# Packing the row-maximum search into 18 visits a group, moving its pairs behind the second products of two chunks, and warming the entries of three stages, in a gated attention and MLP kernel on one Trainium2 core

## The reference, cut to what matters

```python
def reference(x, w_qkv, w_out, W1, B1, W2, B2, LN_G, LN_B):   # x: (4, 1024, 256) float32
    xn = layernorm(x)
    # attention: 16 heads of 16 dims, causal, over 4 sequences of 1024
    q, k, v = split(xn @ w_qkv); q = q / 4
    scores = where(causal, q @ k.T, -1e10)
    s = (softmax(scores) @ v) @ w_out
    # MLP: 6 blocks, hidden width 1024
    y = xn
    for i in range(6):
        y = gelu(y @ W1[i].T + B1[i]) @ W2[i].T + B2[i] + y
        if i < 5: y = layernorm(y) * LN_G[i] + LN_B[i]
    return x + s * silu(y)
```

## Time and profile before

| what | us |
|---|---|
| median of three runs | 1572.16 |
| the profiled execution, its own time | 1569.95 |
| span of its records | 1568.2 |
| PE busy in the span | 1539.3 (98%) |
| DVE busy | 1227.6 (78%) |
| ACT busy | 959.3 (61%) |
| POOL busy | 384.8 (25%) |

### The profile page before, as it was taken

One profiled execution on the slowest core, in us unless ns is written; L12 is line 12 of the kernel. 1 busy time (PEld: TensorE's weight loads), 2 busy tenths in 40 slices (PEclk: granted clock), 3 DMA queues, 4 the chain that ended last, 5 costly groups with the idle time before them and its releaser, 6 DMA issues. The chain is left out here.

```text
span 1568.2 us, 28737 instructions
## 1 busy us (share of the span) xinstructions
PE 1539.3 (98%) x10960; PEld 1196.9 (76%) x10960; DVE 1227.6 (78%) x2688; ACT 959.3 (61%) x1404; POOL 384.8 (25%) x325
## 2 busy tenths in 40 slices
PE   7989999999999999999999999999999999999998
PEld 6879888888888888888888888888888644444443
DVE  7835988888889888879898898887666487777742
ACT  4455655565555555555656555555545599898985
POOL 2002322222212222223222222221110222333333
PEclk9999999999999999999999999999999899999999
DMA  9868546547545214232132142131610355456441
GB/s 309 319 204 243 152 122 181 151 119 195 138 118 114 69 36 115 66 93 69 47 102 69 44 115 66 38 103 53 186 56 28 108 143 170 141 180 180 114 133 45
DMA packets 110145, 193.37 MB, mean 123 GB/s; under 512 B 13644, under 2 KB 80716, under 8 KB 102348
## 3 DMA queue, kind: packets, MB, share of 16 engines
q1 hardware_dynamic: 110008, 191.54, 42.3%
HBM read 136.70 MB, written 79.95 MB: 138 GB/s over the span
## 5 line engine op out<-in xcount | busy, mean ns | idle before, releaser
L759 ACT ACTIVATE m_hid<-m_h_ps,m_b1s 128x512 f32<-128x512 f32 x384 | 264.7, 689 | 490.4 <-PE m_h_ps L862 456.2
L834 DVE TENSOR_TENSOR m_hidl<-m_hid,m_hidh 128x512 fp32r<-128x512 f32 x384 | 358.7, 938 | 184.4 <-ACT m_hidh L762 173.5
L1093 ACT ACTIVATE a_prob<-a_st_ps 128x1024 f32<-128x1024 f32 x288 | 277.6, 1023 | 36.1 <-PE a_st_ps L1164 31.4
L875 PE MATMUL m_y_ps<-shared,m_hidh 128*128 128x256 f32 x1536 | 273.8, 281 | 0.5 <-DVE xres L793 0.5
L762 ACT ACTIVATE m_hidh<-m_h_ps,m_b1s 128x512 fp32r<-128x512 f32 x384 | 261.6, 681 | 0.0
L862 PE MATMUL m_h_ps<-xth,shared 128*128 128x512 f32 x768 | 254.3, 392 | 3.7 <-ACT m_hidh L762 2.0
L875 PEld LDWEIGHTS m_y_ps<-shared,m_hidh 128*128 128x128 f32 x1536 | 234.8, 188 | 19.0 <-issue 14.6
L875 PE MATMUL m_y_ps<-w2h,m_hidh 128*128 128x256 f32 x768 | 219.0, 285 | 0.7 <-DVE xres L793 0.7
L875 PE MATMUL m_y_ps<-w2l,m_hidh 128*128 128x256 f32 x768 | 212.7, 277 | 0.0
L875 PE MATMUL m_y_ps<-shared,m_hidl 128*128 128x256 f32 x768 | 212.7, 277 | 0.0
L875 PE MATMUL m_y_ps<-w2h,m_hidl 128*128 128x256 f32 x768 | 212.7, 277 | 0.0
(11 more groups left out here) (116 smaller groups left out, 2583.8 us busy)
## 6 DMA issues: line engine op xcount, KB each, us to landing
turned_rows<-apart SPq DMA_DIRECT2D x47, 512.0 KB, 2.7
apart<-turned_rows SPq DMA_DIRECT2D x188, 128.0 KB, 3.1
mq<-q_stacks SPq DMA_DIRECT2D x16, 896.0 KB, 6.9
mk<-k_stacks SPq DMA_DIRECT2D x16, 896.0 KB, 10.1
shared<-k_stacks SPq DMA_DIRECT2D x14, 896.0 KB
shared<-q_stacks SPq DMA_DIRECT2D x14, 896.0 KB
q_stacks<-q_parts SPq DMA_DIRECT2D x96, 128.0 KB
k_stacks<-k_parts SPq DMA_DIRECT2D x96, 128.0 KB
```

What stands on the lines that cost most here:

```text
L759: nc.scalar.activation(hid[n % 2][:], h_ps[n % 2][:], ACT.Gelu, bias=b1s[i % 2][:, k:k + 1])
L834: nc.vector.tensor_tensor(hidl[n % 4][:], hid[n % 2][:], hidh[n % 4][:].bitcast(F32), ALU.subtract).then_inc(low_done, 1)
L875: m = nc.tensor.matmul(y_ps[:, j, :], h[n % 4][:, j * P:(j + 1) * P], w[par][:, k, :], start=(k == 0 and j % 2 == 0 and h is hidh and w is ...
L1093: nc.scalar.activation(to, scores, ACT.Exp).then_inc(exp_done, 1)
```

## The change

It has these parts.

1. `max_pieces` packs two pieces with a diagonal into one visit where they fit in a buffer: 18 visits a group, with the same matmuls and the same reductions. 189 visits, in 95 places, are in stage 2, and 115 in stage 3, over the same 124 steps (none shares a step).
2. In stage 2 PE takes a place's pair behind `down(n-2)`, `down(n-1)`, and DVE takes it one chunk later.
3. The six products of `up` stand in another order.
4. Stage 1: the weights come in three column parts; PE does 16 transposes of `ident` ahead of `transpose0` and 12 behind it; the biases of MLP block 0 are loaded here; the Gelu table is asked for here, and the one for Exp at the end of stage 2's ACT list.
5. Stage 3: in steps 0 and 1, where there are no `values` yet, PE does four matmuls of 512 columns for nothing (`keep_awake`); `values` waits for each diagonal apart; of the last eight output tiles the first goes ahead of the last `values`, and four use the score buffers, so that tiles 1 to 5 wait for no earlier one.

```diff
 def max_pieces():
...
-    pieces = []
-    for qt in range(QT):
-        for half in range(1 + qt // HG):
-            keys = min(P * (qt + 1) - BANK * half, BANK)
-            columns = min(BANK // keys, PAIR)
-            pieces += [(qt, half, c, columns, keys) for c in range(0, PAIR, columns)]
-    return pieces
+    def own(qt, c, col=0):
+        return qt, qt // HG, c, P * (qt % HG + 1), col
+
+    def far(qt, c):
+        return qt, 0, c, BANK, 0
+
+    both = range(PAIR)
+    pieces = [[own(2, c), own(0, c, BANK - P)] for c in both] + [[own(1, c, BANK // 2 * c) for c in both]]
+    pieces += [[own(3, c)] for c in both] + [[far(4, c)] for c in both]
+    pieces += [[own(6, c), own(4, c, BANK - P)] for c in both] + [[far(5, c)] for c in both]
+    pieces += [[own(5, c, BANK // 2 * c) for c in both]] + [[far(6, c)] for c in both]
+    return pieces + [[far(7, c)] for c in both] + [[own(7, c)] for c in both]
...
 def project(nc, x, wqkv, w1t, w2t, b1, b2, scratch, keep):
-        WCOLS = [slice(0, 2 * DIM), slice(2 * DIM, 3 * DIM)]
+        WCOLS = [slice(DIM * part, DIM * (part + 1)) for part in range(3)]
...
+            load_bias(sp, keep, b1, b2, 0)
...
             low(0)
             split_w(1)
+            split_w(2)
             statistics(1)
...
+            act.preload_act_table(ACT.Gelu)
             high_w(0)
             high(0)
             high_w(1)
+            high_w(2)
...
+            def keep_awake(times):
+                for j in range(times):
+                    nc.tensor.transpose(v_ps[:, 0, 0:P], ident[:], ident[:])
+
+            keep_awake(16)
             transpose0()
+            keep_awake(12)
...
 def mlp(...):
-            load_bias(0)
...
-            act.preload_act_table(ACT.Gelu)
...
+            act.preload_act_table(ACT.Exp)
...
-                for v in AT.get(n, ()):
+                for v in AT.get(n - 1, ()):
                     search.dve_visit(dve, s_ps[v % 2], v)
...
-                for c in range(HALVES):
-                    for w, x in ((w1h, xth), (w1h, xtl), (w1l, xth)):
+                products = ((w1h, 0, xth), (w1h, 0, xtl), (w1l, 1, xth), (w1l, 0, xth), (w1h, 1, xtl), (w1h, 1, xth))
+                for order, (w, c, x) in enumerate(products):
...
-                for v in AT.get(n, ()):
-                    search.pe_visit(pe, s_ps[v % 2], v, 2)
                 if n >= 2:
                     down(n - 2)
                     down(n - 1)
+                for v in AT.get(n, ()):
+                    search.pe_visit(pe, s_ps[v % 2], v, 2)
...
 def output_schedule():
-            at, bank = copied_at(N_GROUPS - 1, 1) + 3 + k // 2, ("s", k % 2)
+            at = copied_at(N_GROUPS - 1, 1) + (3 + k if k else -1)
+            bank = (("s", 0), ("s", 1), ("st", 0), ("st", 1), ("st", 2), ("st", 3), ("s", 0), ("s", 1))[k]
...
 def attend(...):
-            act.preload_act_table(ACT.Exp)
...
+                    if P * kt == lo:
+                        selected += 1
+                        pe.wait_ge(masked, selected)
...
+            def keep_awake():
+                for j in range(HG):
+                    nc.tensor.matmul(o_ps[0][2 * HD * j:2 * HD * (j + 1), :], va[0][:, 0, j, :], xres[:, 0:2, :], start=True, stop=True,
+                                     skip_group_check=True)
...
+                if at < LATE:
+                    keep_awake()
```

More of the change, by code:

```diff
@@ L188, in pe_visit @@
             pe.wait_ge(s.loaded[m % 2], 2 * 16 * (m // 2 + 1))
-        qt, half, first, columns, keys = PIECES[p]
-        for c in range(columns):
+        for part, (qt, half, c, keys, col) in enumerate(PIECES[p]):
             for side in range(2):
-                if c == 0 and before > 0:
+                if part == 0 and before > 0:
                     pe.wait_ge(s.maxed, before - 1 + side)
                 rows = slice(SIDE * side, SIDE * side + STACK)
-                i = s.nc.tensor.matmul(s_ps[:, side, c * keys:(c + 1) * keys], s.q[m % 2][rows, first + c, qt * P:(qt + 1) * P],
-                                       s.k[m % 2][rows, first + c, half * BANK:half * BANK + keys], start=True, stop=True)
+                i = s.nc.tensor.matmul(s_ps[:, side, col:col + keys], s.q[m % 2][rows, c, qt * P:(qt + 1) * P],
+                                       s.k[m % 2][rows, c, half * BANK:half * BANK + keys], start=True, stop=True)
         i.then_inc(s.done, 1)
```

48 lines of the change are left out of this document (27 added, 21 removed).

## The result

The changed kernel takes 1563.09 us (median of four, 1562.50 to 1566.81); the kernel before, run beside it, 1572.03. The ratio is 0.9948, with a 95% interval from 0.9935 to 0.9961: 0.5% faster where 0.9% was forecast, 1563.1 where 1557.5 stood, inside the range (1554 to 1563.5) by 0.4 us and far from its centre. The profiled execution took 1563.66 us with a span of 1561.8; before 1569.95 and 1568.2. So of 14.7 us forecast 6.4 appear in the span. Where they went can be read place by place.

What follows compares the result with a forecast made beforehand. It took PE's instructions to bound stage 2 and ACT's exponents ordinary stage 3 steps. Terms −4.0 + 0.7 − 2.0 − 4.4 − 3.3 − 1.7 gave −14.7 us: 1555.2 profiled, 1557.5 median, range 1554 to 1563.5 (8 in 10).

Steps and rivals of the forecast that it cites:

- start of stage 1: Transposes of group 1 come later because DVE's list has two weight splits ahead of the statistics: +0.7 us, bounds +0.3 and +0.7.
- entry −2.0: Entry of stage 2: with biases and Gelu table loaded early, PE no longer waits before the third chunk: −2.0 us.
- packing −4.0: Stage 2: ten of 105 places go, each costing 0.40 us beyond its columns: −4.0 us.
- place 0: Stage 2: moving the pair behind the second products costs nothing, taken as 0 within −4 to +4 us.
- entry of stage 3: Earlier table load saves 0.8 us and idle matmuls holding the clock save 3.65 us: −4.4 us.
- doubles in stage 3: No step has two visits any more, so steps 41 and 82 lose no time on ACT: −3.3 us.
- the end: Last output tiles: PE ends near 1562, then POOL's seven adds set the end at 1563.9: −1.7 us.
- the clock of stage 3 falls anyway: Rival: the entry of stage 3 gives +1.0 us instead of −4.4, total 1562.9 us; chance 0.20.
- a wait for the buffers: Rival: in stage 2 PE waits for DVE's late reductions in some 32 places, 1570 to 1589 us; 0.07 slower, 0.07 about even.
- rounds with a pair over 6.4 us: Sign that the forecast is wrong: stage 2 rounds with four 512-column matmuls were to still take 6.35 us.
- the rival that they wake it: Rival: stage 1's transposes raise PE's clock, so the start loses 0.3 us and not 0.7, total 1557.1 us; chance 0.12.
- the places give nothing back: Rival: in stage 2 the new place costs 0.04 us more, 95 times, eating packing's 4.0 us, total 1561.5 us; chance 0.10.

Runs made afterwards that it cites:

- best: Changed kernel with column loads ahead of the search's DMAs, group 1's statistics ahead of two weight splits, 8 idle transposes before group 1's transposes: 1557.03 us.
- no_packing: Changed kernel with the 20 pieces a group of the kernel before, instead of 18: 1567.59 us, ratio 0.9979.
- control: The changed kernel run once more, nothing edited: 1561.15 us, ratio 0.9933.
- stage3_cold: Changed kernel without the eight idle matmuls in steps 0 and 1 of stage 3: 1564.03 us, ratio 0.9953.
- columns_first: Changed kernel with the four column loads of every slot issued ahead of the search's loads and stores on SP: 1557.93 us, ratio 0.9906.
- start_cold: Changed kernel without the 28 idle transposes of stage 1: 1560.14 us, ratio 0.9928.
- best_bufs: The kernel of best with four output buffers for pairs of tiles instead of three: 1555.76 us, ratio 0.9901.
- before_columns: The kernel before the change, with column loads ahead of the search's DMAs on SP: 1569.96 us, ratio 0.9989.
- old_up_order: Changed kernel with the six first products of a chunk (`up`) in their old order: 1562.67 us, ratio 0.9941.
- run 114: Not a run label: "run" is a verb here, and 114 or 118 ns is the spacing of second products.

## Why the prediction was wrong, step by step

Each step as forecast, in the first profile, and in best (differences to the profile of before; those of stage 3 from the starts of the exponents):

| step | forecast | first profile | best |
|---|---|---|---|
| start of stage 1 | +0.7 | +1.75 | −0.30 |
| stage 2: entry −2.0, packing −4.0, place 0 | −6.0 | −0.30 | −6.26 |
| entry of stage 3 | −4.4 | −4.2 | −4.2 |
| doubles in stage 3 | −3.3 | −3.3 | −3.3 |
| the end | −1.7 | −1.9 | −0.4 |
| not forecast, stage 3 | 0 | +1.6 | +1.5 |
| span | −14.7 | −6.4 | −13.0 |

**The terms for work removed were right in size, two sums of them partly by luck.** The entry of stage 2 (2.0 us), packing (3.7 us in no_packing against the control), the doubles and the entry of stage 3 came within 0.4 us each. But in the entry of stage 3 the clock was over-sized (1.7 us for 3.65 in stage3_cold) and the rest under-sized (2.5 for 0.8). And stage 2 of best, −6.26 for −6.0, is 2.2 us from ahead of the third chunk of slot 3 (the entry), 1.9 from waits of the kernel before that the forecast did not count (for DVE's sum and at the turn), and only 2.2 from shorter instructions, where 4.0 stood: the new place costs back some 1.8. The rival that the clock of stage 3 falls anyway is out, that of a wait for the buffers too: in stage 2 PE waited for L215 or L220 once, at a turn. The sign "rounds with a pair over 6.4 us" was touched: the 14 rounds in the stretch with a pair of eight matmuls take 6.42 us in the control (median), those with four or six 6.25 and 6.30.

**The step that failed first is the reading of stage 2 as "a sum of PE's instructions", so that "only what shortens PE's list, or a wait at its entry, moves it".** The stretch before slot 3 was already at its limit in the kernel before: columns converted at 152.17, low part over just before 154.54, product at 154.54. I saw a busy PE and not that a transfer ended in the same instant. In the first profile the columns were 2.4 us later and cost the stall and a fall of the clock, 3.9 us together by the starts of slot 3's third chunk (161.01 before, 164.68 after, at +3.67 where slot 2 stood at −0.24). Issuing them earlier took that away, and the wait of the turn with it: 3.2 us by the medians of columns_first and the control, of the 3.7 that lay between the control and the forecast.

**The start was mis-sized: +1.75 us for +0.7.** I took the transposes to run at half clock ("the row says otherwise"), with 0.12 for the rival that they wake it. They do: with them the full clock came at 4.9 to 11.5 us in all 14 executions profiled, without them at 15.0, 15.4 and 17.2. Start_cold differs from the control in these transposes alone, and its clock was full only at 15.4 us. The Trainium skill (TensorE: Matmul & The Clock Gate, Part 4) says that transposes do not count as work for the clock; here the measurement differs and decides. DVE's chain was summed rightly: without the early clock stage 2 started at +0.65 (start_cold), and the early clock brought the 0.4 us (the low part at 9.42 for 9.86, the transposes of group 1 at 16.34 for 16.77), which gave +0.11 in the control. What was missing is that PE's first products were over 2 us sooner and DVE's chain only those 0.4, and that behind the 2.55 us hole so made the clock fell, in four executions of seven, for 1.64 us. I had looked at who waits at 16.18 and not at how long the wait becomes when the waiting engine is made faster.

**The end came right in the first profile by chance, and hid a new wait.** The last two tiles wait for a store three pairs back: 0.91, 1.21 and 2.41 us in three executions, and with the last of them −1.9 us is −0.4 in best. I had counted PE and POOL only; best_bufs gave 1.3 us for a fourth buffer. The sign named for the end, 8 us between the last exponent and the last add, did not follow from its own sum either, which ends at 1563.9, 10.1 us behind the last exponent of the kernel before (1553.79); 9.9 was measured.

**Not forecast** are step 122 (+0.9 by step 125: the last turn waits for DVE) and two drifts of 0.36 us. And "the places give nothing back" was weighed as a loss of 0.04 us a place; what happens is 115 ns on the first products behind a visit in the new place for 97 on the second ones in the old, a pace (27 to 63 slow rounds in the new place for 7 to 20 in the old, 77 ns each), and fewer waits for DVE, which together come to nearly nothing.

**The median.** The sum was made against one execution and carried over by adding 2.2 us. But those 2.2 us are losses of single executions of the kernel before. Which ones is not shown, as it has one profile; the fall at the entry of stage 2 in before_columns is one that the change removes, while it brings in others. Against the medians, best is 14.5 us faster than before (1557.03 to 1571.55), nearly the forecast of 14.7, with the losses of chance gone on one side and the edits of the repairs added, so it does not bear the sum out.

## What to carry to other kernels

Where an engine is busy throughout, look at what arrives just in time for it: a transfer or a chain that ends in the same microsecond as it is wanted is a wait as soon as anything is made faster. Compute for every wait that you leave standing how long it becomes once the engine in front of it is quicker, since the hole can cost its length and then the clock behind it. And take two or three profiles before trusting differences of 4 us in 1560: here one showed two falls of the clock that the next did not have.

## What was unexpected of the hardware

- fp32 transposes of 128 columns raised TensorE's clock: full at 6.3 us behind 16 of them from 2.0 us on in the first profile, at 4.9 to 11.5 us in the others with them, at 15.0, 15.4 and 17.2 us without.
- At holes of 2.13 to 2.81 us in PE's work the clock fell to 0.5 for 3.4 us in seven of the ten cases in stages 1 and 2, and not in the other three, with the same hole of 2.54 us on both sides; at the many of 0.5 to 2.05 us it fell once (old_up_order, at a turn that waited 1.73 us near 717).
- At one and the same granted clock second products run 114 or 118 ns apart, a pace that is mostly kept over many rounds and changes at a visit.
- Behind a visit (matmuls on 48 rows) the next run of full-height products takes 97 ns more if it is 24 of 256 columns, 115 if it is 12 of 512 (2.86 us for 2.75).
